# Two key tiles of values at a time, and another order for the first stacks, in a three-layer softmax attention

## The reference, cut to what matters

```python
x = x + attention(layernorm(x), ctx)          # L0x: keys and values from the context
x = x + gated_attention(layernorm(x))         # L0f: from x itself, queries normalised, output gated
x = x + attention(layernorm(x), ctx)          # L1x

def attention(q, kv):                         # all float32
    qh, kh, vh = heads(q @ Wq.T + bq), heads(kv @ Wk.T + bk), heads(kv @ Wv.T + bv)
    attn = softmax(einsum('nqhd,nkhd->nhqk', qh, kh) / 4.0)
    return merge(einsum('nhql,nlhd->nhqd', attn, vh)) @ Wo.T + bo
```

## Time and profile before

| | us |
|---|---|
| runs | 4552.01, 4549.38, 4552.75 |
| median | 4552.01 |
| profiled execution | 4549.59 |
| its span, first to last instruction | 4547.6 |
| PE busy, whole span | 4283.4 (94%) |
| DVE busy | 2994.0 (66%) |
| ACT busy | 2515.0 (55%) |

### The profile page before, as it was taken

One profiled execution on the slowest core, in us unless ns is written; L12 is line 12 of the kernel. 1 busy time (PEld: TensorE's weight loads), 2 busy tenths in 40 slices (PEclk: granted clock), 3 DMA queues, 4 the chain that ended last, 5 costly groups with the idle time before them and its releaser, 6 DMA issues. The chain is left out here.

```text
span 4547.6 us, 65866 instructions
## 1 busy us (share of the span) xinstructions
PE 4283.4 (94%) x23716; PEld 2379.6 (52%) x23750; DVE 2994.0 (66%) x7431; ACT 2515.0 (55%) x5640; POOL 810.0 (18%) x550
## 2 busy tenths in 40 slices
PE   5999999999999998779898999999999998999999
PEld 2333343433333333458544666666666666556555
DVE  4777677777677775978685676776766666344333
ACT  2666666656566666543464767677776766111111
POOL 2323335353323220532100000000000000000000
PEclk7999999999999999899898999999999999999999
DMA  7464463535354550100101110101101001000000
GB/s 141 73 86 74 61 84 68 70 56 75 54 83 68 76 84 23 42 10 19 75 1 33 31 32 26 36 27 31 31 27 36 29 29 69 8 5 5 10 5 10
DMA packets 182839, 204.92 MB, mean 45 GB/s; under 512 B 44651, under 2 KB 165099, under 8 KB 180854
## 3 DMA queue, kind: packets, MB, share of 16 engines
q1 hardware_dynamic: 182518, 200.72, 24.2%
HBM read 139.90 MB, written 60.78 MB: 44 GB/s over the span
## 5 line engine op out<-in xcount | busy, mean ns | idle before, releaser
L479 DVE TENSOR_REDUCE L0x_maxes<-L0x_ps_max 128x1 f32<-128x512 f32 x1536 | 988.6, 685 | 297.4 <-PE L0x_ps_max L745 296.1
L661 ACT ACTIVATE L0x_probs<-L0x_ps_sc 128x1024 f32<-128x1024 f32 x768 | 778.0, 1026 | 421.7 <-PE L0x_ps_sc L734 416.0
L745 PE MATMUL L0x_ps_max<-L0x_kstack,L0x_qstack 96*128 96x512 bf16 x1536 | 590.7, 385 | 27.3 <-DVE L0x_maxes L479 22.6
L2736 ACT ACTIVATE L3x_pexp<-L3x_ps,L3x_nmax 128x77 f32<-128x77 f32 (+2 forms) x1536 | 601.3, 433 | 0.0
L734 PE MATMUL L0x_ps_sc<-L0x_qstack,L0x_kstack 104*128 104x512 bf16 x1536 | 523.0, 382 | 11.0 <-ACT L0x_probs L661 6.5
L2618 DVE TENSOR_REDUCE L3x_nmax<-L3x_ps 128x2 f32<-128x154 f32 (+2 forms) x768 | 346.6, 507 | 241.8 <-PE L3x_ps L2849 239.4
L756 PE MATMUL L0x_ps_out<-L0x_probs,L0x_vpad 128*32 128x512 f32 x3072 | 411.5, 608 | 9.0 <-ACT L0x_heads_raw L669 8.6
L2744 ACT COPY L3x_pT<-L3x_ps 128x512 f32<-128x512 f32 x512 | 275.1, 593 | 225.8 <-PE L3x_ps L2857 225.4
L2236 ACT ACTIVATE L3f_act_g<-L3f_ps_gu 128x512 f32<-128x512 f32 x128 | 76.4, 597 | 542.1 <-PE L3f_ps_gu L2282 542.0
L745 PEld LDWEIGHTS L0x_ps_max<-L0x_kstack,L0x_qstack 96*128 96x128 bf16 x1536 | 149.1, 97 | 418.0 <-DVE L0x_maxes L479 322.2
L2634 DVE TENSOR_SCALAR L3x_pexp<-L3x_pexp,L3x_rsum 128x77 f32<-128x77 f32 (+2 forms) x1536 | 358.1, 307 | 6.8
(11 more groups left out here) (377 smaller groups left out, 6778.1 us busy)
## 6 DMA issues: line engine op xcount, KB each, us to landing
L0x_kstack<-parts_scratch SPq DMA_DIRECT2D x144, 256.0 KB, 10.0
L0x_qstack<-parts_scratch SPq DMA_DIRECT2D x144, 256.0 KB, 14.8
parts_scratch<-L0x_kparts SPq DMA_DIRECT2D x24, 768.0 KB, 3.7
parts_scratch<-L0x_qparts SPq DMA_DIRECT2D x24, 768.0 KB, 5.0
rel_scratch<-L3x_rel_e SPq DMA_DIRECT2D x32, 408.0 KB, 2.4
L3x_rel_d<-prob_scratch SPq DMA_DIRECT2D x32, 408.0 KB, 3.1
L0x_kv_in<-in_ctxT SPq DMA_DIRECT2D x16, 512.0 KB, 4.5
L3x_rel_t<-rel_scratch SPq DMA_DIRECT2D x32, 154.0 KB, 2.4
```

The source lines that it names most:

```text
L479: V.tensor_reduce(maxes[:, t, head:head + 1], ps_max[:, unit % 2, :], AX.X, ALU.max).then_inc(max_taken, 1)
L661: nc.scalar.activation(probs[:, n % 4], ps_sc[:, 2 * (n % 2):2 * (n % 2) + 2, :], ACT.Exp, scale=HD ** -0.5).then_inc(probs_ready, 1)
L745: nc.tensor.matmul(ps_max[:, unit % 2, :], qstack[q.parity][0:ROWS, head, t * P:(t + 1) * P], kstack[q.parity][0:ROWS, head, :], start=Tru ...
L2736: i = nc.scalar.activation(pexp[:, n % 4, e, a:b], ps[:, SB + 2 * (n % 2) + e, a:b], ACT.Exp, bias=nmax[:, n % 4, s, e:e + 1], accum_out=s ...
```

## The change

Four things change, all in `softmax_attentions`.

1. `values` now runs at steps with n % 4 = 1 and takes two key tiles: eight matmuls in place of four. `probs` grows from 4 slots to 6 to hold the steps between, and is numbered over all items. The semaphore `probs_used` counts per four steps.
2. Within a step the order is score, maximum, score, maximum in all steps but the one behind the values (n % 4 = 2), which keeps maximum, score, score, maximum.
3. `vpad` puts the heads 17 floats apart (16 values and a one). A load of 32 columns then reads into the neighbour's columns, whose results land in rows of `ps_out` that nobody uses.
4. At the start, the values of item 0 are projected in pass -2 behind the queries, the second context is loaded ahead of the query stacks, and ACT issues every second one of the first twelve stack DMAs.

```diff
+FIRST = [(2, "k", 0), (3, "k", 1), (14, "xnT", 0), (18, "xnT", 1), (24, "q", 0), (26, "q", 1), (29, "v", 0),
+         (30, "v", 1)]
...
+    SLOTS = 6
+    PER = 4
...
-        vpad = [ph.sb(f"vpad{b}", [P, TILES, HEADS, 32], F32) for b in range(2)]
+        vpad = [ph.sb(f"vpad{b}", [P, TILES, HEADS * (HD + 1) + 15], F32) for b in range(2)]
...
-        probs = ph.sb("probs", [P, 4, 2, S], F32)
+        probs = ph.sb("probs", [P, SLOTS, 2, S], F32)
...
-                    if m == n and q.number + shift(w, c) == x.number]
+                    if m == n and q.number + shift(w, c) == x.number and (x.later or w != "v")]
...
+        def stack_rows(engine, q, here, part_of, stack, r):
+
+            engine.dma_start(stack[q.parity][HD * r:HD * r + HD, :, :],
+                             scratch[here, part_of[r]].rearrange("c (h d) s -> d (c h) s", d=HD)
+                             ).then_inc(stack_in, 16)
...
-                for r, part in enumerate(part_of):
...
+                for r in range(len(part_of)):
+                    if q.later or r % 2 == 0:
+                        stack_rows(sp, q, here, part_of, stack, r)
...
-                if q.number == -1:
-                    sp.wait_ge(q_out, nxt.count(16, 16))
-                    stacked(nxt, 1, q_part, qstack)
                 if ahead.there and ahead.cross and ahead.later:
                     if nxt.cross:
                         sp.wait_ge(taken["v"], nxt.count(2, 2))
                     context(ahead)
+                if nxt.there:
+                    sp.wait_ge(q_out, nxt.count(16, 16))
+                    stacked(nxt, 1, q_part, qstack)
                 if q.number == -1:
                     for b in range(2, SEQS):
                         load_sequence(sp, T, G, b)
                     load_weights("L0f", "mixture")
-                if q.number >= 0 and nxt.there:
-                    sp.wait_ge(q_out, nxt.count(16, 16))
-                    stacked(nxt, 1, q_part, qstack)
...
-                if n % 2 == 0 and (q.later or n >= 4):
-                    act.wait_ge(probs_used, q.count(STEPS // 2, n // 2 - 1))
-                nc.scalar.activation(probs[:, n % 4], ps_sc[:, 2 * (n % 2):2 * (n % 2) + 2, :], ACT.Exp,
+                at = q.count(STEPS, n)
+                if at >= SLOTS and (at - SLOTS) % PER == 0:
+                    act.wait_ge(probs_used, (at - SLOTS) // PER + 1)
+                nc.scalar.activation(probs[:, at % SLOTS], ps_sc[:, 2 * (n % 2):2 * (n % 2) + 2, :], ACT.Exp,
...
+                if q.number == -1:
+                    for here, part_of, stack, out in ((0, k_part, kstack, k_out), (1, q_part, qstack, q_out)):
+                        act.wait_ge(out, 16)
+                        for r in range(1, len(part_of), 2):
+                            stack_rows(act, Item(0), here, part_of, stack, r)
...
-                for j in range(4):
-                    i = nc.tensor.matmul(ps_out[32 * j:32 * j + 32, :], vpad[q.parity][:, kt, 4 * g + j, :],
-                                         probs[:, (pairs + j // 2) % 4, j % 2, :], start=(kt == 0),
-                                         stop=(kt == TILES - 1), tile_position=(0, 32 * j))
+                for k in range(2):
+                    kt = first % 8 // 2 + k
+                    for j in range(4):
+                        head = 4 * g + j
+                        i = nc.tensor.matmul(ps_out[32 * j:32 * j + 32, :],
+                                             vpad[q.parity][:, kt, (HD + 1) * head:(HD + 1) * head + 32],
+                                             probs[:, q.count(STEPS, first + 2 * k + j // 2) % SLOTS, j % 2, :],
+                                             start=(kt == 0), stop=(kt == TILES - 1), tile_position=(0, 32 * j))
                 i.then_inc(probs_used, 1)
...
-                    if n % 2 == 1 and q.there:
+                    behind_values = n % PER == 2
+                    if not behind_values and q.there:
                         score(q, n, 0)
                     if own.there:
                         for_maximum(own, 2 * (m % STEPS))
-                    if n % 2 == 0 and q.there:
+                    if behind_values and q.there:
                         score(q, n, 0)
...
-                    if n % 2 == 1 and (q if n > 1 else q.plus(-1)).there:
-                        values(q if n > 1 else q.plus(-1), (n - 3) % STEPS, q.there)
+                    if n % PER == 1 and (q if n > 1 else q.plus(-1)).there:
+                        values(q if n > 1 else q.plus(-1), (n - 5) % STEPS, q.there)
```

17 lines of the change are left out of this document (7 added, 10 removed).

## The result

The changed kernel takes 4567.1 us (median of 10 runs, 4558.9 to 4568.3) against 4552.4 of the kernel before (10 runs): ratio 1.003, interval 1.0021 to 1.0040. It is 15 us slower, a third of a per cent. The profiled execution took 4567.56 us (span 4565.5) in place of 4549.59.

The account below looks back on a forecast made before the run. PE was taken as the bound, with waits for DVE inside its sum. From the profiled 4549.6 us, the start gives -12.4 and the passes +23: 4560 us, range 4522 to 4590.

Parts of the forecast that it names:

- The double group: Eight value matmuls for two key tiles, run together: 1.86 us to the next start, against 1.00 for a single group.
- Rival 2: Value matmuls on PE: the eight do not stream and cost 2.00, not 1.86; +27 us, 4587; chance 0.13.
- DVE takes it back: With two ps_max banks DVE idles during long value groups; PE's saving becomes waiting, +1.1 us per cross-attention pass.
- The walk through the places of a cross pass: Step-by-step estimate over a pass among cross-attention items, stretches from +0.65 to -0.3 us, sum +1.1 us.
- 10 to 13: Steps 10 to 13 of a cross-attention pass: DVE's gapless chain sets the length, values still start at 8.4; +0.65 us.
- rival 1: PE alone decides: the value-group saving arrives wholly (46 us, 4494) or half (4517 to 4540); chance 0.24.
- The start: Program start: first maximum at 61.3 in place of 73.71 us, -12.4 us (-9 to -13.5), not given back later.
- 28 + 27 + 4 + 1.5: Start: ACT's key-stack issue at 28, plus 27, query parts 4, context 1.5: all stacks in at about 60.5 us.
- PE's chain: Start: ACT's copies, then two projections at half clock with a copy between, ready at 60.6 us.
- the mixture passes: Full passes with mixture items: gate place 1.1 us shorter, everything else 1.5 longer, +0.4 us each.
- without the group at 23 this place is 1.1 us shorter: Step 23 of mixture passes, where PE waits 2.99 us for DVE's gate chain: removing its value group saves 1.1 us.
- rival 4: Gates, step 23: a shorter wait (2.6, not 2.99) might keep the clock up; -8 us, 4552; no chance given.

Follow-up runs that it names:

- the halved pair: The kernel before and the changed kernel, both with every maximum reduced over 256 of its 512 keys: 4525.3 us and 4462.3 us.

## Why the prediction came out right

*The double group* was put at 1.86 and costs 1.86. Rival 2 (2.00) is out. The rows that carried it were those of another stage: float32 matmuls that follow each other in one tiled form.

*DVE takes it back*: shown by the halved pair, where the sign turns. The walk through the places of a cross pass came within 0.15 us at every row of the table above, and its price within 0.2 (+1.26 measured, +1.1 forecast). That is partly luck: 10 to 13 was +0.86 for +0.65 and 14 to 17 -0.39 for -0.3, two errors that partly cancel. The maxima stand 0.60 apart in strict alternation, and the values of step 13 start 8.40 after the projection. A saving of rival 1's size came only where a reduction took 0.42 us in place of 0.68, and there 0.8 us a pass belongs to the wait for ACT's copy.

*The start*: first maximum at 60.53 and 61.84 in two executions, forecast 61.3. It came near partly by luck. I gave ACT's queue 4 us and the rest to the order; with the queue taken away from the changed kernel 11 us are lost and 2 stay. Two queues with the old order were not run, so this split holds only for that sequence. The sum "28 + 27 + 4 + 1.5" has two steps that the trace contradicts: ACT issues its key stacks at 30.67, not at 28, and the last key stack lands at 48.49, where 28 + 13.4 + 4 is 45.4. And the rate isn't flat: context and query stacks land by 60.13, 11.6 us later, where 13.4 + 1.5 is 14.9. The two errors of some 3 us offset each other. PE's chain was also as late as I had said, and both end together (the last query stack 0.4 us before the first maximum, 60.13 and 60.53).

*The term that failed* is the mixture passes: +0.4 each forecast, +1.6 in this profile, 6 of the missing 9 us. The step is "without the group at 23 this place is 1.1 us shorter". The place before, in pass 10 (TensorE's timeline):

```profile
857.69 0.39 PE L745 MATMUL L0x_ps_max<-L0x_kstack,L0x_qstack 96*128 96x512 bf16 x1 [2.99 <-DVE L0x_maxes L479]
...
858.61 1.07 PE L756 MATMUL L0x_ps_out<-L0x_probs,L0x_vpad 128*32 128x512 f32 x8
859.61 1.99 PE L776 MATMUL L0x_ps_t<-L0x_wo_mixture,L0x_hT 128*128 128x256 f32 x8
861.44 0.38 PE L745 MATMUL L0x_ps_max<-L0x_kstack,L0x_qstack 96*128 96x512 bf16 x1
```

and after, in pass 11:

```profile
936.25 0.61 PE L757 MATMUL L0x_ps_max<-L0x_kstack,L0x_qstack 96*128 96x512 bf16 x1 [2.99 <-DVE L0x_maxes L484]
...
937.51 3.62 PE L792 MATMUL L0x_ps_t<-L0x_wo_mixture,L0x_hT 128*128 128x256 f32 x8
940.92 0.63 PE L746 MATMUL L0x_ps_sc<-L0x_qstack,L0x_kstack 104*128 104x512 bf16 x1
...
942.20 0.45 PE L757 MATMUL L0x_ps_max<-L0x_kstack,L0x_qstack 96*128 96x512 bf16 x1
942.49 0.60 PE L830 MATMUL L0x_ps_t<-ident,L0x_heads_raw 128*128 128x128 f32 x4
```

Two things were wrong. First, I read one such place and took its length for all five; two of the five ran at full clock (the projection above takes 1.83) and last 14.04, not 15.68. Second, I priced the low clock at the 1.64 us it cost in the earlier trace rows. The wait is 2.99 in both kernels; rival 4 and its shorter wait had no ground, since the group that goes stands behind the wait. After the change the clock is already at 1.2 GHz when TensorE resumes at 936.25 and stays there to about 942.2: maxima and scores 0.43 apart, projection 3.41. The granted clock of this stretch (windows view of after, columns as in Rows 1):

```profile
936.30:942.10 5.80, 5.80 (x14) 3.43 (x15) 2.74 (x6) 1.02 (x1) 5.64 (x4) 0.50 0.24 84
```

and of the one before in pass 10:

```profile
857.70:861.40 3.70, 3.70 (x19) 1.89 (x20) 1.73 (x3) 1.02 (x1) 3.62 (x3) 1.00 0.41 140
```

0.50 is 1.2 GHz, 1.00 is 2.4. The low stretch costs 2.34 (15.55 against 13.21, the shortest such place seen with double groups and full reductions), the removed group is worth 0.83 (14.04 against 13.21): against a place of 15.68 that is -0.83 + 2.34 - 1.64 = -0.13, the -0.10 of the table, and against one of 14.04 it is +1.51. Why the clock is low after the change when the same wait of 2.99 us ends, and was not in pass 10 before, stays open.

The cross passes' missing 2.4 us are 0.9 in item 0 and small change elsewhere; the passes that leave the mixture layer 1.2.

The forecast total was 4560, the median 4567: inside the range, 7 us above the point (the passes lost 9 us more than forecast, the start gave 1.2 more), and on the side that had the largest chance, slower by over 0.2%.

## What to carry to other kernels

Before fewer or longer instructions are bought for the busiest engine, count what its partner can do in the stretch that gets longer: with two banks between them, the partner finishes two pieces and idles, and the time comes back at its own pace (0.60 us a maximum here). A busy share of 98% says nothing about it; the distances between starts do. And where a ledger shows which places gain, an item that reaches over the boundary (here 0.86 us of a group) must be booked to the place that opens it before one picks the good places out.
